# Graph network kernel: in the building of the counts, ScalarE builds the destination one-hots by a square and a relu, in a loop of its own

## What is computed

```
x = layernorm(x + L0(x))   # mean over in-neighbours, projections, features of the last edge of each node
x = layernorm(x + L1(x))   # three attention layers over edges and self-loops
x = layernorm(x + L2(x))   # mean over in-neighbours
x = layernorm(x + L3(x))   # a message for each edge, added up by node
```

## Time and profile before

| what | value |
|---|---|
| median of 3 runs | 5350.39 us (5347.95 to 5350.52) |
| the profiled execution | 5350.4 us, its span 5348.6 us |
| mean granted TensorE clock | 0.918 of full speed |
| busy: PE, DVE, ACT, POOL | 4615.0, 3798.2, 1823.8, 1990.0 us |
| the stage of the counts | from 105 to about 1625 us of the span |
| ACT busy in that stage | 79.46 us of 1520 |

### The profile page before, as it was taken

The page is one execution under the profiler, slowest core; times in us unless marked ns, Lnnn a source line. Parts: engine busy times, 40 slices in busy tenths (PEclk is TensorE's granted clock), DMA queues, the critical chain, the costliest instruction groups (busy, mean ns, idle before and its releaser), DMA issues.

```text
span 5348.6 us, 118073 instructions
## 1 busy us (share of the span) xinstructions
PE 4615.0 (86%) x41659; PEld 3580.5 (67%) x41660; DVE 3798.2 (71%) x5768; ACT 1823.8 (34%) x3064; POOL 1990.0 (37%) x1717
## 2 busy tenths in 40 slices
PE   6999999888886969999579999588886888888886
PEld 3998888888885555555479999564544555555554
DVE  6988888877771057777466666455114999999998
ACT  0000000000001527777337777336341333333332
POOL 3888888882002057100000000000004766666663
PEclk6999999999996879999789999789777999999998
DMA  1000000000000000000000000000001111111113
GB/s 51 6 6 5 5 5 5 5 5 1 0 0 2 0 10 10 4 2 2 20 3 4 4 4 4 17 2 11 1 3 39 37 36 36 36 36 36 36 37 25
DMA packets 203918, 74.19 MB, mean 14 GB/s; under 512 B 169275, under 2 KB 189578, under 8 KB 203658
## 3 DMA queue, kind: packets, MB, share of 16 engines
q0 software_dynamic: 52448, 31.60, 3.5%
q1 hardware_dynamic: 151338, 40.69, 3.5%
HBM read 57.25 MB, written 14.88 MB: 13 GB/s over the span
## 4 chain that ended last, share of the span: by engine, by line
PE 63%; DVE 23%; issue 8%; DVEq 3%; DMA 2%; ACT 1%; POOL 0%; SPq 0%; ACTq 0%; POOLq 0%
PE ps L1182 62%; DVE adj L1140 8%; DVE adj L1132 5%; DVE scratch L851 5%; DVEq L849 1%; DVEq L336 1%; DVE adj L1145 1%; DMA r_dram<-adj 0%; DMA hwork<-gat_out_a 0%; DMA hwork<-gat_out_b 0%; DVE hwork L849 0%; ACT scratch L555 0%; DVE adj L1125 0%; DMA scratch<-gat_out_c 0%; PE ps L1365 0%
## 5 line engine op out<-in xcount | busy, mean ns | idle before, releaser
L1182 PE MATMUL ps<-hwork,scratch 128*125 128x125 bf16 (+1 forms) x25750 | 1931.0, 236 | 99.8 <-DVE scratch L851 90.6
L1182 PEld LDWEIGHTS ps<-hwork,scratch 128*125 128x125 bf16 (+1 forms) x25750 | 1853.0, 151 | 171.6 <-DVE scratch L851 121.8
L1055 DVE SCALAR_TENSOR_TENSOR scratch<-scratch,cols,adj 125x625 f32<-125x625 f32 x1125 | 964.8, 871 | 366.9 <-ACT scratch L641 358.4
L504 POOL DMA_INDIRECT by_src<-work x782 | 1102.5, 1410 | 262.4 <-issue 224.3
L641 ACT ACTIVATE scratch<-work,cols 125x625 f32<-125x625 f32 x1125 | 1003.9, 907 | 305.4 <-PE ps L1182 242.3
L533 POOL DMA_INDIRECT adj<-r_dram,adj x832 | 808.3, 972 | 496.9 <-DMA adj<-by_src 256.1
L851 DVE TENSOR_SCALAR scratch<-hwork,edge_ids 128x3125 bf16<-128x3125 uint16 x830 | 890.3, 1073 | 0.0
L1182 PE MATMUL ps<-scratch,X 125*65 125x375 f32 (+1 forms) x3000 | 825.3, 435 | 4.8 <-DVE scratch L1055 2.7
L1182 PEld LDWEIGHTS ps<-scratch,X 125*65 125x65 f32 x3000 | 415.6, 140 | 396.1 <-issue 286.0
L519 POOL IOTA adj<- 128x125 uint16 x1 | 0.2, 246 | 1813.9 <-DVEq L1104 1813.9
L1182 PEld LDWEIGHTS ps<-adj 128*125 128x125 f16 (+3 forms) x4320 | 386.1, 158 | 419.1 <-issue 380.9
(11 more groups left out here) (253 smaller groups left out, 3075.1 us busy)
## 6 DMA issues: line engine op xcount, KB each, us to landing
adj<-r_dram,adj POOLq DMA_INDIRECT x832
adj<-q_dram SPq DMA_DIRECT2D x416, 31.2 KB
by_src<-work POOLq DMA_INDIRECT x782
by_src<-adj SPq DMA_DIRECT2D x1, 4165.0 KB
adj<-by_src SPq DMA_DIRECT2D x104, 40.0 KB, 2.0
work<-in_rec SPq DMA_DIRECT2D x46, 85.0 KB
gat_out_a<-hwork SPq DMA_DIRECT2D x5, 312.5 KB
hwork<-gat_out_a SPq DMA_DIRECT2D x1, 1562.5 KB
```

The source lines that it names most:

```text
L504: g.indirect_dma_start(by_src, bass.IndirectOffsetOnAxis(ap=pos_now[:, h, k:k + 1], axis=0), rec_in[:, h, k, :], None).then_inc(rec_sent[h ...
L1055: v.scalar_tensor_tensor(slots[:, j % SLOTS, :], slots[:, j % SLOTS, :], cols[:, 2, j, h:h + 1], adj3[:, j, ds(b * BW, BW)], ALU.add, ALU. ...
L1182: return t_.matmul(o_, l, r, start=start, stop=stop, skip_group_check=skip)
```

## The change

ScalarE gets the inner loop, too, and builds `onehot_dst` in two instructions: the square of (destination - iota) into `off_sq` in f32, then relu(1 - square) into `onehot_dst` in bf16, which is 1 where the two are equal and else 0. VectorE no longer builds it. The destinations as f32 (`dst_f`) come from one more cast on VectorE at the start. ScalarE waits for `oh_used` and for the `lastmax` step of chunk n-2, and between its two instructions for the first of them. TensorE waits for `ohd_built` beside `oh_ready`. ScalarE's one-element copy is moved ahead of the loop over windows. `last_chain` starts one higher, and the waits on it are raised to fit.

```
+        dst_f = hflat[0:CH, 2100:2100 + NCH]
+        off_sq = hflat[0:CH, 2900:2900 + 2 * T].rearrange("p (c n) -> p c n", c=2)
...
             act.wait_ge(srt["stored"], 48)
+            a.copy(small[0:1, 60:61], ones[0:1, 0:1]).then_inc(table_loaded, 1)
+            act.wait_ge(table_loaded, 1)
+            act.wait_ge(tab_ready, 1)
+            act.wait_ge(iotas, 2)
+            act.wait_ge(ids_ready, 2)
             with act.Fori(0, NT) as w:
-
-                a.copy(small[0:1, 60:61], ones[0:1, 0:1]).then_inc(table_loaded, 1)
-                act.wait_ge(table_loaded, w + 1)
-
+                k0, k1, back = (tab_load(act, i, w) for i in range(3))
+                with act.Fori(k0, k1) as k:
+                    g = act.snap(...)
+                    for c in range(PAIR):
+
+                        act.wait_ge(oh_used, k * PAIR + c + 1)
+                        act.wait_ge(last_chain, k * PAIR + w + c + 1)
+                        a.activation(off_sq[:, c, :], iota[:, ds(w * T, T)], ACT.Square, bias=dst_f[:, ds(g * PAIR + c, 1)], scale=-1.0).then_inc(off_ready, 1)
+                        act.wait_ge(off_ready, k * PAIR + c + 1)
+                        a.activation(onehot_dst[:, c, :], off_sq[:, c, :], ACT.Relu, bias=ones[:, 0:1], scale=-1.0).then_inc(ohd_built, 1)
...
             v.tensor_copy(edge_ids[:], ids_p).then_inc(ids_ready, 1)
+            v.tensor_copy(dst_f, ids_p[:, 1, :]).then_inc(ids_ready, 1)
...
             dve.sem_inc(oh_used, PAIR)
+            dve.sem_inc(last_chain, 1)
...
                         dve.wait_ge(oh_used, k * PAIR + c + 1)
-                        v.tensor_scalar(onehot_dst[:, c, :], iota[:, ds(w * T, T)], edge_ids[:, 1, ds(g * PAIR + c, 1)],
-                                        None, ALU.is_equal).then_inc(ohd_built, 1)
                         v.tensor_scalar(onehot_src[:, c, :], iota, edge_ids[:, 0, ds(g * PAIR + c, 1)],
                                         None, ALU.is_equal).then_inc(oh_ready, 1)
 
                         dve.wait_ge(ohd_built, k * PAIR + c + 1)
-                        dve.wait_ge(last_chain, k * PAIR + w + c + 1)
+                        dve.wait_ge(last_chain, k * PAIR + w + c + 2)
...
                         pe.wait_ge(oh_ready, k * PAIR + c + 1)
+                        pe.wait_ge(ohd_built, k * PAIR + c + 1)
...
-                pe.wait_ge(last_chain, w + k1 * PAIR + 1)
+                pe.wait_ge(last_chain, w + k1 * PAIR + 2)
```

More of the change, by code:

```diff
@@ L222, in build_gnn @@
             sem("tabc_ready"), sem("tab_ps"), sem("tab_ready"))
-        oh_ready, oh_used, ohd_built, last_chain = sem("oh_ready"), sem("oh_used"), sem("ohd_built"), sem("last_chain")
+        oh_ready, oh_used, ohd_built, last_chain, off_ready = sem("oh_ready"), sem("oh_used"), sem("ohd_built"), sem("last_chain"), sem("off_ready")
         adj_summed, last_turned, last_col = sem("adj_summed"), sem("last_turned"), sem("last_col")
@@ L543, in _ @@
             act.wait_ge(srt["stored"], 48)
-            with act.Fori(0, NT) as w:
-                a.copy(small[0:1, 60:61], ones[0:1, 0:1]).then_inc(table_loaded, 1)
-                act.wait_ge(table_loaded, w + 1)
+            a.copy(small[0:1, 60:61], ones[0:1, 0:1]).then_inc(table_loaded, 1)
[3 more added lines that the diff above has]
+            act.wait_ge(ids_ready, 2)
+            with act.Fori(0, NT) as w:
+                k0, k1, back = (tab_load(act, i, w) for i in range(3))
+                with act.Fori(k0, k1) as k:
+                    g = act.snap(nc.s_assert_within(k - back, 0, NG - 1, skip_runtime_bounds_check_because="a window's steps lie in 0 to NG"))
+                    for c in range(PAIR):
[4 more added lines that the diff above has]
+                        a.activation(onehot_dst[:, c, :], off_sq[:, c, :], ACT.Relu, bias=ones[:, 0:1], scale=-1.0).then_inc(ohd_built, 1)
                 act.wait_ge(adj_summed, w + 1)
```

## The result

The changed kernel takes 5257.86 us (median of 3 runs, 5255.87 to 5261.5), the kernel before 5350.39. Its profiled execution took 5261.5 us, with a span of 5259.7.

The account below looks back on a forecast made before the run. Bound: the ring, 3.28 us a pair, by neither engine's sum. 201 pairs x (0.17 - 0.03) = 28, 164 x 0.07 = 11.5, window starts 4, cast -1: together 43, rounded to 45 off 5350, so 5305 us; range 5265 to 5370.

Parts of the forecast that it names:

- the ring: Chunk buffers: TensorE's matmuls free one, VectorE refills it, TensorE starts again; 3.28 us a pair, for 365 pairs.
- What leaves: VectorE's refill: without L849 0.17 us leaves, a pair of 3.11 us; at most 62 us, and 4 at window starts.
- A: Way from buffer free to buffer filled: 1.61 us before; forecast 1.44 for VectorE, 1.35 for ScalarE.
- TensorE's 3.11 us as a floor: TensorE's 50 matmuls of a pair, with their end, take 3.11 us.
- rival (d): VectorE's refill: L849's register steps go too (0.05 and 0.05), a pair of 3.01, 98 us gained, 5252 us; chance 0.09.
- What ScalarE adds: ScalarE's two instructions: 0.43 + 0.387 + 0.10 + 0.387 + 0.05 = 1.35 us, covered by VectorE's 1.44.
- (a): ScalarE's refill about as late as VectorE's was: 1.52 to 1.66 us, middle about 5345 us; chance 0.13.
- (b): ScalarE's refill slower, with five more register steps: 1.78 us, a pair of 3.45, 5412 us; chance 0.13.
- New waits: TensorE's added wait costs 0.03 us in the ring; L856, waiting for ScalarE, can slip about 0.1 us, free on most pairs.
- halving the gain there: Stretch of GpSimd's DMAs: slow L851 (+0.21 us) may close the ring, so 164 pairs gain 0.07 us each.
- rival (c): ScalarE's loop: a table load of 1.283 us a pair, a pair of 4.30, 5773 us; chance 0.03.
- the cast to `dst_f`: Added cast of 128 x 782 in a serial stretch of VectorE: +1 us at most.

Follow-up runs that it names:

- after_dst_twice: The changed kernel with VectorE also building the destination one-hot, into a buffer that nothing reads: 5359.64 us.
- before_no_dst: The kernel before with the destination one-hot built once ahead of the loop, not in it, and without ScalarE's part: 5220.25 us.
- no_dst_half_src: The kernel before without the destination one-hot in the loop and with the source one-hot over 1560 columns only: 5190.68 us.
- after_half_src: The changed kernel with the source one-hot built over its first 1560 columns only: 5242.89 us.
- before_dst_static: The kernel before with VectorE still building the destination one-hot in each chunk, but from fixed addresses: 5231.33 us.
- after_act_late2: The changed kernel with a copy of 128 x 125 f32 on ScalarE ahead of each square: 5274.22 us.

## Why the prediction was wrong

**What bounds the kernel** was right: the ring, not an engine's sum. after_dst_twice brought it back by giving VectorE's way its 0.52 us again.

**The step that failed: "What leaves".** It counted L849 at the 0.17 us between two starts and kept the whole 0.35 us from TensorE's end to VectorE's start as if they were a fixed time to wake up. They were L849's own register steps, in good part: the 0.19 of DVEq stood in the earlier trace rows. With the instruction they went too: in before_no_dst the first instruction behind the signal, the source one-hot, starts after 0.17 us. before_no_dst gives 2.951 - 1.67 = 1.28 us for VectorE's A, where the prediction had 1.44: a term of 0.16 us, 56 us over 352.5 pairs, was missing. The window's start shows the same: the source one-hot starts 0.30 us after the memset (1400.69 to 1400.99), where it was 0.66 before; the borders gave 11 us where 4 were forecast.

**TensorE's 3.11 us as a floor** was the second half of the same error. It contains the tail of the last matmul, which overlaps with the next chunk when that is ready. The floor is 2.895 (no_dst_half_src). The weight loads' 2.97 for 50, named in rival (d) and not followed, pointed there.

**What ScalarE adds** was nearly right, and then not used. A of 1.35 gives 1.67 + 1.35 = 3.02 us a pair; after_half_src, where VectorE's way is short, has 3.023. But it was called covered by VectorE's 1.44, and as VectorE's is 1.28 by itself, ScalarE is the later one. In the changed kernel VectorE's is 1.35, too, because L869 waits for the relu and holds the next source one-hot back. That the sum for ScalarE came out is partly luck. The parts: 0.40 ahead of the square (0.43 forecast), 0.40 for each instruction (0.387 forecast), 0.03 between them (0.10 forecast), and 0.11 to TensorE behind them (0.05 forecast). Rivals (a) and (b) had its direction, ScalarE in the ring, but they measured it against the wrong 1.61; rival (d), with the chance 0.09, named what happened: the register steps go with L849. That its 98 us lie near the 92.5 is luck. It let 0.10 us of register steps go, where 0.16 went, and it had VectorE's ring set the pair, not ScalarE's. Its 5252 us also lies below the stated range of 5265 to 5370, though the prediction says that the range leaves out only its end.

**New waits.** TensorE's second wait costs nothing where it is satisfied early (0.03 forecast); behind ScalarE's one-hot its instruction stands in the 0.11 us. L869 slips by 0.2 to 0.3 us on one of the two chunks, not 0.1; with after_half_src's 3.023 against 3.044 it is worth about 0.02 us a pair at most. **GpSimd:** slow source one-hots became fewer (53 over 1.15 us, 164 before), so halving the gain there was wrong: the pair gained as much with the DMAs (3.269 to 3.050 in the first twelve windows) as without (3.242 to 3.027).

**Right as forecast:** the cast to `dst_f` takes 0.56 us, the vanished table loads give nothing, and rival (c) didn't happen. Up to the end of this stage ScalarE has one table load; the nine later ones of the program were there before:

```profile
L546 ACT ACT_TABLE_LOAD  x1: 1283/1283/1283, 89.2 to 89.2; - x1
```

The page "ScalarE: Activation LUTs" of the Trainium skill (Table sets: the hidden batching unit) leaves square out of its list of what is in every set; here the set that the copy loads serves copy, square and relu. The page's rule to keep such functions on VectorE (Rules for kernel authors) holds by duration, 0.80 against 0.28 us, but not for this ring, where ScalarE runs beside VectorE; before_dst_static shows that VectorE could have kept the work if its addresses had been ready.

## What to carry to other kernels

In a loop with computed addresses, count register steps between a wait and the instruction behind it as part of that instruction; when it leaves, they leave. The time to wake up isn't a constant. Before moving work to another engine, try the same instruction with fixed addresses: here that alone was worth 119 of the 130 us that removing it was worth.

A ring over a buffer has as many ways as engines that fill it, and the later one counts. An engine that waits for another's result ahead of its own next buffer passes the delay on. Compare each with the others after the change, not with the time before it, and take a floor of a pipelined engine from its rate without the last instruction's tail.

## What the runs showed of the hardware that was not expected

- Two computed addresses of one small VectorE instruction cost 0.295 us a pair. Without them the instruction costs 0.017, as it covers the register steps of the one behind it (before_dst_static beside before_no_dst and before).
- An instruction of 0.30 us put ahead of one with computed addresses delays that one by 0.02 us where it started 0.40 us after its signal, and by 0.10 where it started after 0.20 (after_act_late2).
- A satisfied semaphore wait on TensorE, one for every 25 matmuls, has no price (5231.3 us with and without).
- TensorE's first weight load follows 0.05 us behind VectorE's one-hot, and 0.11 behind ScalarE's where the second wait is the last (after_half_src); no run parts the wait from the signal's way.
- TensorE at a granted clock of 1.00 shows itself busy for 180.00 of 180 us while each pair is 5% longer than it can go: a gap under the length of a matmul record (0.23 us) is not seen in its busy time. The starts of the weight loads, 0.058 us apart without a stall, show it.
